# A gated cross-attention and expert kernel: gathered rows normalised by ScalarE, splits between product copies, and no unread products around the rank

## What is computed

```
x = x + tanh(g_xattn[0]) * attention0(layernorm(x), ctx)
x = x + tanh(g_ffn[0])   * experts(layernorm(x))
x = x + tanh(g_xattn[1]) * attention1(layernorm(x), ctx)
x = x + tanh(g_ffn[1])   * fp8_linear(layernorm(x))

logits = x @ gate_w.T + expert_bias;  w = softmax of the top 2
h_e = silu(x @ w1[e].T);  y_e = h_e @ w2[e].T
out = sum over the two experts e of w_e * y_e  (or w_e * x)
```

## Time and profile before

| | |
|---|---|
| median of 3 runs | 374.53 us (371.19 to 375.9) |
| the profiled execution | 375.71 us |
| its span | 373.9 us |
| mean granted clock of TensorE | 0.97 |
| TensorE busy | 339.3 us, 91% of the span |
| VectorE busy | 274.6 us, 73% |
| ScalarE busy | 209.5 us, 56% |
| GpSimd busy | 161.8 us, 43% |

### The profile page before, as it was taken

The page is one execution under the profiler, slowest core; times in us unless marked ns, Lnnn a source line. Parts: engine busy times, 40 slices in busy tenths (PEclk is TensorE's granted clock), DMA queues, the critical chain, the costliest instruction groups (busy, mean ns, idle before and its releaser), DMA issues.

```text
span 373.9 us, 8932 instructions
## 1 busy us (share of the span) xinstructions
PE 339.3 (91%) x2879; PEld 267.1 (71%) x2880; DVE 274.6 (73%) x729; ACT 209.5 (56%) x432; POOL 161.8 (43%) x211
## 2 busy tenths in 40 slices
PE   4999975856999999999999998889999999999995
PEld 2777843635989999999999983556667666666674
DVE  2579987868576766765665657868888988867796
ACT  2589883213354454454454442466767787775586
POOL 7098984288355555555655444321131232101100
PEclk9999987888899999999999999989999999999999
DMA  6999963011122222223323214310111000000005
GB/s 177 326 403 423 424 228 85 16 42 28 58 72 72 77 78 72 83 69 75 81 70 73 68 44 141 114 58 4 58 58 41 19 2 1 4 2 2 1 31 196
DMA packets 15339, 36.21 MB, mean 97 GB/s; under 512 B 3526, under 2 KB 6748, under 8 KB 13772
## 3 DMA queue, kind: packets, MB, share of 16 engines
q1 hardware_dynamic: 10508, 24.66, 18.1%
q0 software_dynamic: 3936, 10.48, 10.2%
q10 hardware_dynamic: 864, 0.66, 0.6%
HBM read 22.28 MB, written 13.52 MB: 96 GB/s over the span
## 4 chain that ended last, share of the span: by engine, by line
PE 73%; DVE 14%; ACT 5%; DMA 4%; issue 2%; POOL 1%; SPq 0%; DVEq 0%
PE two L1980 15%; PE two L1995 14%; PE two L2132 5%; PE two L2162 5%; PE two L2014 4%; PE two L2197 4%; PE two L2118 4%; PE two L2098 3%; PE two L2005 2%; DVE xq L1377 2%; PE two L2189 2%; DVE stat L1093 2%; DMA x_sb<-in_x 1%; PE two L1864 1%; PE two L2178 1%
## 5 line engine op out<-in xcount | busy, mean ns | idle before, releaser
L859 ACT ACTIVATE th<-two 128x512 f32<-128x512 f32 x39 | 23.3, 597 | 73.4 <-PE two L1995 44.5
L613 POOL DMA_INDIRECT y_d<-y_sb,goal_i x39 | 38.6, 989 | 53.2 <-ACT y_sb L869 53.2
L1388 DVE SCALAR_TENSOR_TENSOR gate<-th,two 128x512 f32<-128x512 f32 x39 | 26.8, 687 | 41.2 <-ACT th L859 23.0
L607 POOL DMA_INDIRECT xg<-xn_d,slot_i x39 | 38.0, 975 | 23.8 <-DVE slot_i L1327 11.3
L1980 PE MATMUL two<-wh,gh 128*128 x156 | 44.7, 287 | 0.1
L1980 PE MATMUL two<-wh,gl 128*128 x156 | 44.2, 283 | 0.0
L1980 PE MATMUL two<-wl,gh 128*128 x156 | 44.1, 283 | 0.0
L636 POOL TENSOR_TENSOR rstd<-var,half 128x2 f32<-128x2 f32 x14 | 9.9, 708 | 76.6 <-DVE var L1458 76.6
L573 POOL TENSOR_TENSOR wl<-wl,wh 128x512 fp32r<-128x512 f32 x32 | 40.2, 1279 | 0.1
L1491 DVE TENSOR_REDUCE nm<-two 128x8 f32<-128x960 f32 x32 | 36.1, 1152 | 5.4 <-PE two L2118 5.0
L1995 PE MATMUL two<-wh,xh 128*128 x78 | 34.8, 446 | 0.4 <-DVE xl L1382 0.4
(11 more groups left out here) (307 smaller groups left out, 859.6 us busy)
## 6 DMA issues: line engine op xcount, KB each, us to landing
wl<-in_wmoe SPq DMA_DIRECT2D x8, 1024.0 KB, 12.1
y_d<-wh SPq DMA_DIRECT2D x4, 1024.0 KB
yg<-y_d SPq DMA_DIRECT2D x7, 512.0 KB, 3.5
xn_d<-x_sb SPq DMA_DIRECT2D x8, 258.0 KB, 7.3
x_sb<-in_x SPq DMA_DIRECT2D x8, 256.0 KB, 5.8
out_x<-of SPq DMA_DIRECT2D x8, 256.0 KB, 2.0
xg<-xn_d,slot_i POOLq DMA_INDIRECT x39
y_d<-y_sb,goal_i POOLq DMA_INDIRECT x39
```

The costliest lines, as they stand in the source:

```text
L607: pool.indirect_dma_start(xg[:, n % 2, :], None, xn_d, bass.IndirectOffsetOnAxis(ap=slot_i[:, n:n + 1], axis=0)).then_inc(gathered[n % 2], 16)
L613: pool.indirect_dma_start(y_d, bass.IndirectOffsetOnAxis(ap=goal_i[:, n:n + 1], axis=0), y_sb[:, n % 2, :], None).then_inc(y_stored[n % 2] ...
L1388: dve.scalar_tensor_tensor(gate[:, k, :], th[:], 1.0, bank[2 + k][:], ALU.add, ALU.mult).then_inc(gate_ok, 1)
```

## The change

The normalisation of the gathered rows (`norm_of`) goes from VectorE to ScalarE, as one activation with the row's factor as its scale and its shift as its bias. In each step it stands on ScalarE behind `xh` of block s + 4 and ahead of the tanh of block s + 3, and is for block s + 5.

Splits 20 to 23 go behind four small instructions on ScalarE, and splits 24 to 31 go one by one behind the copies of the products 0 to 7.

On TensorE products 4 to 8 go ahead of the rank, products 9 to 11 behind it, all ahead of the slot products; two unread products ahead of the rank and four behind it are left out. In the two steps that start with block 2 and 3, the transposes of that block go behind the first products of the block before (`rows_last`).

```
--- before.py
+++ after.py
@@ -753,10 +753,6 @@
                     act.wait_ge(zeroed, 16 * ZERO_LOADS)
                 c = cols(j, CHUNK)
                 nc.scalar.activation(wh[:, c], wl[:, c].bitcast(F32), ACT.Copy).then_inc(split_h, 1)
-
-            def highs(lo, hi):
-                for n in range(lo, hi):
-                    high(n)
 
             def highs(lo, hi):
                 for n in range(lo, hi):
@@ -824,7 +820,6 @@
             copy_probT(6)
             exp0_of(7)
             copy_probT(7)
-            highs(20, CHUNKS)
             nc.scalar.activation(less_ident[:], ident[:], ACT.Copy, scale=-1.0)
             nc.scalar.activation(rows_are[:], count[:].unsqueeze(2).to_broadcast([P, P, 2]), ACT.Copy, scale=-1.0)
             nc.scalar.activation(cols_are[:], count[:, 0:BLOCKS].unsqueeze(2).to_broadcast([P, BLOCKS, 2]), ACT.Copy,
@@ -834,9 +829,9 @@
                 ins = nc.scalar.activation(token16[:, cols(k, TILES // 2), :].rearrange("p t k -> p (t k)"),
                                            token[:, cols(k, TILES)], ACT.Identity, scale=1.0 - 2 * k, bias=unit[:, k:k + 1])
             ins.then_inc(iota_ok, 1)
-            act.wait_ge(con_in, IN_CON)
-            act.wait_ge(pv_done, B)
-            for n, (what, m, h) in enumerate(P1):
+
+            def keep_product(n):
+                what, m, h = P1[n]
                 act.wait_ge(p1_mm, n + 1)
                 if what == "kt1":
                     half_of = kt1[:].rearrange("p (b c k) -> p b c k", b=B, c=C)[:, h * B // 2:(h + 1) * B // 2, m, :]
@@ -845,8 +840,23 @@
                                          bias=bk1_sb[:, m:m + 1]).then_inc(p1_act, 1)
                 else:
                     nc.scalar.activation(v1[:, m * D:(m + 1) * D], p1_bank(n)[0:LK, 0:D], ACT.Copy).then_inc(p1_act, 1)
+
+            highs(20, 24)
+            act.wait_ge(con_in, IN_CON)
+            act.wait_ge(pv_done, B)
+            for n in range(CHUNKS - 24):
+                keep_product(n)
+                high(24 + n)
+            for n in range(CHUNKS - 24, len(P1)):
+                keep_product(n)
             act.wait_ge(dif_ok, 1)
             nc.scalar.activation(ex[:], dif[:], ACT.Exp).then_inc(ex_ok, 1)
+
+            def norm_of(i, k):
+                act.wait_ge(gathered[k], 16 * (i + 1))
+                wait(act, xgT_done, 2 * i + k - 1)
+                nc.scalar.activation(xq[:, k, :], xg[:, k, 0:D], ACT.Identity, scale=xg[:, k, D:D + 1],
+                                     bias=xg[:, k, D + 1:D + 2]).then_inc(xq_ok, 1)
 
             def xh_of(i, k):
                 wait(act, xgT_done, 2 * i + k + 1)
@@ -871,6 +881,8 @@
             def slot(i, k):
                 if live(i, k, 4):
                     xh_of(*ahead_of(i, k, 4))
+                if live(i, k, 5):
+                    norm_of(*ahead_of(i, k, 5))
                 if live(i, k, 3):
                     th_of(*ahead_of(i, k, 3))
                 if live(i, k, 0):
@@ -882,7 +894,11 @@
                 slot(i, 0)
                 slot(i, 1)
 
-            for i in range(-2, 1):
+            norm_of(0, 0)
+            norm_of(0, 1)
+            xh_of(0, 0)
+            slot(-2, 1)
+            for i in range(-1, 1):
                 pair(i)
             with act.Fori(1, PAIRS - 3) as i:
                 pair(i)
@@ -1371,12 +1387,6 @@
                 then(dve.tensor_scalar(red[:, 7:8], red[:, 5:6], FP8_MAX, FP8_MAX, ALU.mult, ALU.min))
                 then(dve.reciprocal(red[:, 9:10], red[:, 7:8]))
 
-            def norm_of(i, k):
-                wait(dve, gathered[k], 16 * (i + 1))
-                wait(dve, xgT_done, 2 * i + k - 1)
-                dve.tensor_scalar(xq[:, k, :], xg[:, k, 0:D], xg[:, k, D:D + 1], xg[:, k, D + 1:D + 2], ALU.mult,
-                                  ALU.add).then_inc(xq_ok, 1)
-
             def xl_of(i, k):
                 wait(dve, xh_ok, 2 * i + k + 1)
                 dve.tensor_tensor(xl[:, k, :], bank[k][:, 0:D], xh[:, k, :], ALU.subtract).then_inc(xl_ok, 1)
@@ -1394,8 +1404,6 @@
             def slot(i, k):
                 if live(i, k, 4):
                     xl_of(*ahead_of(i, k, 4))
-                if live(i, k, 5):
-                    norm_of(*ahead_of(i, k, 5))
                 if live(i, k, 3):
                     gate_of(*ahead_of(i, k, 3))
                 if live(i, k, 2):
@@ -1412,10 +1420,7 @@
                     t = 2 * i + (k - 4)
                     dve.tensor_scalar(x_tile(t), x_tile(t), keep_x[:, cols(t, 1)], add_x[:, cols(t, 1)], ALU.mult, ALU.add)
 
-            norm_of(0, 0)
-            norm_of(0, 1)
-            xl_of(0, 0)
-            slot(-2, 1)
+            pair(-2)
             pair(-1)
             for n, (i, k) in enumerate(((0, 0), (0, 1), (1, 0), (1, 1))):
                 slot(i, k)
@@ -1934,8 +1939,7 @@
             products1(0, 3)
             pe.wait_ge(x1_done, B)
             busy(bank[3], 2)
-            products1(3, 4)
-            busy(bank[3], 2)
+            products1(3, 9)
             pe.wait_ge(pairs_ok, 1)
 
             pm, W = pairs[:].rearrange("p t e -> p (t e)"), P + E_FFN
@@ -1945,8 +1949,7 @@
                 ins = pe.matmul(bank[2][:, n * E_FFN:W], tri[:, P:2 * P], pm[:, 0:W - n * E_FFN], start=False,
                                 stop=n == TILES, skip_group_check=True)
             ins.then_inc(rank_done, 1)
-            products1(4, 10)
-            busy(bank[5], 4)
+            products1(9, len(P1))
             for n in range(4):
                 pe.wait_ge(onerow_ok, n + 1)
                 for m in range(8):
@@ -1956,7 +1959,6 @@
                 ins.then_inc(onerow_used if n < 3 else slots_done, 1)
                 if n < 3:
                     busy(bank[5], 1)
-            products1(10, len(P1))
             def experts(i):
 
                 e = pe.value_load(blk_i[0:1, cols(i, 1)], min_val=0, max_val=E_FFN ** 4 - 1)
@@ -2019,7 +2021,8 @@
 
                 y, h, x, g = live(i, k, 0), live(i, k, 3), live(i, k, 4), live(i, k, 2)
                 (hi, hk), (xi, xk), (gi, gk) = ahead_of(i, k, 3), ahead_of(i, k, 4), ahead_of(i, k, 2)
-                if x:
+                rows_last = x and not y and (i, k) in ((-1, 0), (-1, 1))
+                if x and not rows_last:
                     wait_x(xi, xk)
                     for c in range(C):
                         x_part(xk, c)
@@ -2033,6 +2036,10 @@
                             wait_y(i, k)
                         y_part(k, e_y, 2 * n)
                         y_part(k, e_y, 2 * n + 1)
+                if rows_last:
+                    wait_x(xi, xk)
+                    for c in range(C):
+                        x_part(xk, c)
                 if g:
                     wait_g(gi, gk)
                     for c in range(FC):
```

56 lines of the change are left out of this document (31 added, 25 removed).

## The result

| | before | changed |
|---|---|---|
| median of 20 runs | 374.78 us (371.19 to 381.21) | 370.78 us (369.22 to 375.68) |
| ratio, 95% interval | | 0.9913 [0.9884, 0.9941] |
| the profiled execution (its span) | 375.71 us (373.9) | 371.73 us (369.7) |
| from the start of the writing of `slot_i` to the transposes of block 6 | 28.43 us | 22.45 us |
| from there to the last gate's transposes, "the loop" below | 120.08 us | 123.23 us |

The changed kernel is faster by 4.0 us by the two medians, and by 0.9% (3.3 us) by the ratio: within 2%, and 2.8 us above the forecast of 368.0. The ratio leaves out the slow runs, those over 1.5% above the fastest of their kernel, three before and one of the changed. The start of the expert loop gave what was forecast. The loop behind it gave half of that back in the profiled execution, where the prediction had put a zero.

The account below looks back on a forecast made before the run. TensorE was taken to bound the running expert loop, VectorE's normalisations held by GpSimd its start. 6.13 (start) + 0.4 (rank) = 6.5 us, other terms 0, gave 368.0 us from a 374.53 median; range 365.4 to 371.5.

Parts of the forecast that it names:

- The start, 6.13 us: Expert loop's start: normalisation on ScalarE ends VectorE's long waits; GpSimd's queue then sets block 6's transposes, 6.13 us earlier.
- the sum: Terms added: 6.13 at the loop's start plus 0.4 at the rank, 6.5 us; block 6's transposes 94.17 against 100.30.
- TensorE 1.84 us ahead of block 6: Loop's start: TensorE would be ready at 92.33, 1.84 us before block 6's transposes at 94.17, and wait for the rows.
- The rival of the falling clock: Wait ahead of block 6: TensorE's clock falls to 0.50, losing 1.86 us; 4.6 us remain, 369.9; chance 0.24.
- The rank, +0.4 us: Products moved around the rank, unread products removed: a gain taken as 0.4 us, between the term's bounds.
- the bounds of -0.7 and 1.1: Rank term: 1.1 us gained if the rank runs at 2.4 GHz; -0.7 if slot products run at 1.2 GHz.
- The 0.61: VectorE's wait between its one-hots for TensorE's slot products, 0.61 us, claimed to vanish.
- The steady loop, "Term: 0": Running expert loop: one more ScalarE instruction per step costs nothing; TensorE stays the bound, step 3.48 us.
- the spare time of 1.14 us: ScalarE in each steady step: normalisation runs 154.05 to 154.64, 1.14 us before ScalarE's next instruction at 155.78.
- the fourth rival: Steady loop: normalisation awaiting its gather delays tanh, output copy, scatter and a later gather in a ring; 382 us, chance 0.03.
- The splits and the rows' order, 0: Later splits hidden by GpSimd's idle 11.35 us; later transposes of blocks 2 and 3 given no term of their own.
- The sum for the splits: ScalarE's splits: sixteen instructions of at most 0.6 us from about 53 end by 63, before GpSimd needs them; term 0.

Follow-up runs that it names:

- e2: Changed kernel with the normalisation alone back on VectorE; ratio to the kernel before 1.0011, 375.16 us.
- e11: e10 with block 6's gather ahead of GpSimd's last four low halves and block 7's between them; 368.5 us, ratio to the kernel before 0.9843.
- e10: e6 with TensorE's old order and unread products around the rank, as in e7; 368.64 us, ratio to the kernel before 0.9838.
- e7: Changed kernel with TensorE's old order around the rank and its unread products restored; 368.76 us (1 run).
- e9: The changed kernel itself executed again, nothing changed; 368.71 us (1 run).
- e6: Changed kernel with gathers seven blocks ahead, each gather of the loop waiting on GpSimd for the next block's first products; 370.6 us.
- e3: Changed kernel with two more, already satisfied register waits ahead of the tanh in ScalarE's loop; 367.77 us (1 run).
- e8: Changed kernel with the later transposes of blocks 2 and 3 and the move of ScalarE's last twelve splits both undone; 369.46 us (1 run).
- e12: Changed kernel with gathers seven blocks ahead, each gather of the loop waiting on GpSimd for VectorE's low halves of the next rows (`xl`); 371.4 us (1 run).
- e13: e11 with VectorE's small instructions on the second choice's weights one step later; 368.17 us, ratio to the kernel before 0.983.
- e5: Changed kernel with gathers seven blocks ahead instead of six, same order on GpSimd otherwise; 370.53 us.
- e1: Changed kernel with ScalarE's expert loop written out, so every semaphore target there is a constant; 370.34 us, ratio to the kernel before 0.987.

## Why the prediction was right and wrong

**The start, 6.13 us: right.** 28.43 - 22.45 = 5.98, and 5.69 and 6.01 in the other two executions. (Block 6's transposes before started at 100.13; the 100.30 of the sum is the chain's. With 100.13 the sum has 5.96.) e2 shows that it needs the normalisation's move. e11 beside e10 shows that GpSimd's queue was the bound where TensorE was early enough: with gather 6 earlier in it, block 6 came at 20.96 and not 22.50.

**TensorE 1.84 us ahead of block 6: wrong in the changed kernel, almost without cost there.** The rival of the falling clock had this place. The clock fell, but earlier than it said, from the rank on. In the profiled execution that cost the cover and not the time, since GpSimd's queue is as late; e7 shows the 1.4 us that come back with the clock. But with the cover gone TensorE can be the later of the two: block 6 came 0.3 us later in e9 and 1.5 later in e6.

**The rank, +0.4 us: wrong in sign.** It is 3.74 - 4.01 = -0.27, inside the bounds of -0.7 and 1.1. The 0.61 became 0.20 as said, but the groups of slot products came 69.53 - 68.63 = 0.90 apart at 0.50 of the clock, and `slot_i` waited for the last. The other half of the higher bound, a rank at 2.4 GHz, did not come in these three executions: the rank took 1.22 or 1.23 us as before. It took 0.77 in e2, e3, e6 and e8, and from `pairs` to `slot_i` these need 9.13 to 9.28 us, against 9.33 to 9.52 with the old order and 9.70 to 9.73 in the other traces with the new one; the granted clock from 62 to 66 us is 1.00 in these four and 0.50 to 0.85 in the others, so the term's sign goes with the clock at the rank. The rule that was weighed there (the Trainium skill, page "TensorE: Matmul & The Clock Gate", section "What's actually happening": the slow clock is the default, recent work lifts it) had the right sign; the trace agrees, 0.50 from 70 to 80 us without the unread products (0.50 and 0.84 in the other two executions) and 1.00 with them. The rows with 1.2 GHz were in the profile; the value taken was nearer to the row with the wait.

**The steady loop, "Term: 0": the step that failed.** It cost 3.15, 0.75 and 0.96 us in three executions. Two readings led there. One was the busy row of 19.98 in 20, from which the prediction took that TensorE "never stands still"; the counts of 269 and 280 instructions from 120 to 160 us show a loss that the busy time does not. The other was the spare time of 1.14 us on ScalarE. The normalisation did fit (in the step shown it ended 0.40 ahead of the products), but the spare time was counted up to the tanh's start as it was before, as if the signal of the products came at their end whatever GpSimd does. The ring of the fourth rival is there, keep_y, scatter, gather, in two steps, but its link is not a landing of over 3.9 us: from a gather's start to a normalisation that waits for it 2.7 to 3.3 us were needed up to block 25, with late tanhs from block 5 on, and 3.6 to 3.9 behind that. It is TensorE's signal, held when a gather ends close to the time at which it is due. In the kernel before, the products ended in turns 0.06 us before and 0.02 us after the end of a gather in nearly every step, and the signals were on time; nothing in the prediction asked what else happens at that moment.

**The splits and the rows' order, 0: right** as far as e8 tells them. The sum for the splits counted 16 instructions where 25 stand, five small ones, twelve splits and the eight copies between them; the last split still ended at 60.75 us, ahead of the 63 of the sum, and GpSimd's idle time of 11.61 us hid it.

**The sum.** For the three executions 5.98 - 0.27 - 3.15 = 2.6, 5.69 - 0.27 - 0.75 = 4.7 and 6.01 - 0.24 - 0.96 = 4.8 us, against 6.5 forecast. In the last two the rank is 0.67 and 0.64 below its +0.4, nearly as much as the loop cost them; in the profiled one the loop is most of it. The medians have 4.0, between them; how many of the timed executions stayed in the slower loop is not known.

**Open** is what holds a signal, why e12's were held while the gather still ran and those of the kernel before were not, and why the state could last when ScalarE normalises: the three kernels with VectorE's normalisation have 3.495 to 3.504 us a step with the same gathers. As ends on TensorE are modelled, a late end of the product itself can't be told from a late signal. That moving the gather removes the late tanhs (e6, and again e10, e11 and e13) and brings them back (e12, one trace) is shown; the path inside the chip is not.

## What to carry to other kernels

A bound engine that reads 100% busy may still run a longer step, as here 3.597 us against 3.495: count its instructions in equal windows before and after, and look at the start of what follows it against the end of what it waits for. When an instruction moves to another engine, what counts is not only whether it fits, but which waits now stand in one queue with it, and whether the ring through them has a second state in which it can stay. Unread products that keep a clock up can pay where they stand (here about 0.3 us) and also through the cover that they give a later stage (1.4 us).

## What the runs showed of the hardware

TensorE's completion signals can reach other engines late while TensorE itself runs on: due 0.05 to 0.4 us after the end of a gather issued by GpSimd they came 0.28 us late at the median and up to 1.83 us, and 1.9 and 3.1 us in e5 while GpSimd ran scatters and gathers close together. In e12 they were also held while a gather ran. ScalarE's and VectorE's signals were never late.

Executions with the same code up to there differ by up to 5 us in when `slot_i` is written (70.1 us in e3, 75.1 in e1), which the expert loop has no part in. The first attention's last product ends at 51.8 us in e3 and at 56.3 in e1, so most of it comes from there; its cause was not looked for. A stage is better judged from an event inside it than from the span.
